# A cross-attention round on one core: both halves of the scores in one run, the exponentials ahead of the output's copy, Wo's product one round later

## What is computed

```python
x = x + cross_attention(ctx, layernorm(x), mask, ...)   # 8 heads of 64; queries from x, keys and values from x and ctx
x = x + int8_linear(layernorm(x))                       # rows quantised to 8 bits, times weight_q
x = x + attention(layernorm(x) @ We, ctx) @ W2.T        # softmax over tokens
x = x + routed_ffn(layernorm(x))                        # argmax of 8 experts, 128 -> 512 -> 128
```

```python
q, k, v = x_hat @ Wq, [x_hat, ctx_hat] @ Wk, [x_hat, ctx_hat] @ Wv
q, k = l2norm(q) * q_scale, l2norm(k) * k_scale      # per head
attn = softmax(where(mask, 8 * q @ k.T, -max))       # 128 queries, 128 + 77 keys, 8 heads
out = layer_norm((attn @ v) @ Wo)
```

## Time and profile before

| | |
|---|---|
| median of three runs | 973.37 us |
| span of the profiled execution | 950.6 us |
| median less the span: what lies around it | 22.8 us |
| TensorE busy, matmuls / weight loads | 96% / 84% |
| VectorE, ScalarE, POOL busy | 78%, 73%, 48% |
| TensorE's granted clock | full in nearly all slices |
| DMA | 31.44 MB, mean 33 GB/s |

### The profile page before, as it was taken

How to read it: one execution, slowest core, us unless ns; L and a number is a source line. 1 busy time by engine, 2 the same in 40 slices (tenths; PEclk the granted TensorE clock), 3 DMA queues, 4 the chain that set the end, 5 groups by cost and what they waited for, 6 DMA issues and landing times.

```text
span 950.6 us, 30821 instructions
## 1 busy us (share of the span) xinstructions
PE 912.8 (96%) x11286; PEld 794.5 (84%) x11286; DVE 744.9 (78%) x2526; ACT 693.5 (73%) x1671; POOL 458.1 (48%) x1094
## 2 busy tenths in 40 slices
PE   7999999999999999999999999999999999899997
PEld 6788888788878887888788878888888878898997
DVE  5566787888888888888888888888888978877553
ACT  4877777677778787778777777777778766676664
POOL 5422433354535453545354444444454545777554
PEclk9999999999999999999999999999999999999999
DMA  7743000000000000000000000000000022245310
GB/s 196 200 124 57 2 2 2 2 13 2 14 2 14 2 14 2 13 3 10 5 10 5 8 8 8 7 8 7 8 8 8 7 47 71 61 97 106 95 55 20
DMA packets 45193, 31.44 MB, mean 33 GB/s; under 512 B 11555, under 2 KB 40166, under 8 KB 45046
## 3 DMA queue, kind: packets, MB, share of 16 engines
q1 hardware_dynamic: 39398, 19.93, 9.2%
q0 software_dynamic: 4320, 8.50, 2.8%
q10 hardware_dynamic: 1328, 1.06, 0.4%
HBM read 17.75 MB, written 12.17 MB: 31 GB/s over the span
## 4 chain that ended last, share of the span: by engine, by line
PE 69%; DVE 14%; ACT 8%; issue 3%; POOL 3%; DMA 1%; SPq 1%; DVEq 0%; POOLq 0%; ACTq 0%
PE ps L1670 9%; PE ps L1717 9%; PE ps L1643 7%; PE ps L1765 6%; PE ps L1450 5%; PE ps L1622 5%; PE ps L1630 5%; PE ps L1452 5%; PE ps L1451 5%; DVE sumsq L1267 4%; PE ps L1722 3%; ACT probs L604 2%; PE ps L1749 2%; ACT qk_hat L617 2%; PE ps L1496 1%
## 5 line engine op out<-in xcount | busy, mean ns | idle before, releaser
L1374 DVE TENSOR_TENSOR qk_hat<-ps,rstd 128x512 f32<-128x512 f32 x168 | 106.3, 684 | 49.2 <-POOL rstd L870 49.1
L1267 DVE TENSOR_REDUCE sumsq<-qk_hat 128x8 f32<-128x512 f32 x168 | 107.8, 677 | 35.9 <-ACT qk_hat L617 34.7
L863 POOL TENSOR_TENSOR rs_t<-rs_y 128x32 f32<-128x32 f32 x73 | 17.9, 245 | 235.2 <-ACT rs_y L658 235.2
L1670 PE MATMUL ps<-v_x,prob 128*64 128x65 f32 x2048 | 127.9, 225 | 2.1 <-ACT w_all L568 0.4
L1670 PE MATMUL ps<-v_c,prob 128*64 128x65 f32 x2048 | 124.2, 222 | 0.0
L677 ACT ACTIVATE prob<-ps,neg_shift 128x512 f32<-128x512 f32 x128 | 88.4, 690 | 48.6 <-PE ps L1717 48.6
L1670 PEld LDWEIGHTS ps<-v_x,prob 128*64 128x64 f32 x2048 | 105.0, 137 | 20.9 <-issue 19.2
L617 ACT ACTIVATE qk_hat<-ps 128x512 f32<-128x512 f32 x168 | 98.5, 599 | 31.7 <-PE ps L1452 25.8
L1450 PE MATMUL ps<-w_hi,xc_hi 128*128 128x512 f32 x272 | 120.8, 444 | 0.8 <-POOL xc_lo L835 0.8
L1717 PE MATMUL ps<-qT_all,kT_all 64*128 64x128 f32 x1536 | 111.6, 285 | 2.3 <-ACT prob L677 1.1
L1452 PE MATMUL ps<-w_hi,xc_lo 128*128 128x512 f32 x272 | 107.3, 395 | 0.0
(11 more groups left out here) (245 smaller groups left out, 2257.2 us busy)
## 6 DMA issues: line engine op xcount, KB each, us to landing
x_res<-sorted_rows SPq DMA_DIRECT2D x71, 65.5 KB, 1.9
w_all<-in_L_ffn_W_dram SPq DMA_DIRECT2D x16, 256.0 KB, 5.3
sorted_rows<-fill SPq DMA_DIRECT2D x8, 327.5 KB
out_dram<-prob,x_res POOLq DMA_INDIRECT x71
sorted_rows<-stage,idx POOLq DMA_INDIRECT x64, 2.4
ctx_res<-in_ctx_dram SPq DMA_DIRECT2D x8, 115.5 KB
x_res<-in_x_dram SPq DMA_DIRECT2D x1, 768.0 KB
sorted_rows<-fill SPq DMA_DIRECT2D x1, 524.0 KB, 5.0
```

The costliest lines, as they stand in the source:

```text
L1267: nc.vector.reduce_sum(sumsq[:, n * H:(n + 1) * H], sq[:, n * INNER:(n + 1) * INNER].rearrange("p (h d) -> p h d", d=DH), AX).then_inc(ss_ ...
L1374: nc.vector.tensor_tensor(qk_hat[:, n * INNER:(n + 1) * INNER].rearrange("p (h d) -> p h d", d=DH), ps_qk[:, n, :].rearrange("p (h d) -> p ...
L1670: last = nc.tensor.matmul(dst[half:half + DH, :], prob[:, kt, col + half:col + half + DH], v, start=kt == 0, stop=kt == 1)
```

## The change

- `scores(1)` now follows `scores(0)` at once. It waits for `on_done` (VectorE has read banks 3 and 4), and its two units go to banks 4 and 3 in place of 4 and 6, so that the four units of scores have four banks.
- Where the context half is made in quarters of the array, the x half is too: 32 matmuls in place of 16. The fence increment between the two forms is gone.
- The flips of `o_n` go to bank 6, behind both halves and behind the first exponential; the flips of `xc_hat` go behind them.
- ScalarE does all four exponentials (0, 1, 3, 2), then `outputs_copied`, then `scaled_tokens`.
- Wo's product of block j-2 is in round j, behind the flips of `qk_hat` and slot a, in place of block j-1's at the end of round j. It waits for `ot_done` and `xct_sb`.
- Slot a waits at its head for the third exponential of the round before (bank 3), or, from block 65 on, for the copy of the output.

```diff
-        ps_v, ps_ot = (ps[:, 6, :], ps[:, 5, :]), ps[:, 3, :]
-        ps_s = (ps[:, 6, :], ps[:, 5, :], ps[:, 4, :], ps[:, 6, :])
+        ps_v = (ps[:, 6, :], ps[:, 5, :])
+        ps_s = (ps[:, 6, :], ps[:, 5, :], ps[:, 4, :], ps[:, 3, :])
...
+        def ps_ot(j, inside):
+
+            return ps[:, 6 if has(j, inside) else 3, :]
...
-                    nc.scalar.activation(o_t[:, :], ps_ot, ACT.Copy).then_inc(ot_done, 1)
+                    nc.scalar.activation(o_t[:, :], ps_ot(j, inside), ACT.Copy).then_inc(ot_done, 1)
...
+                if has(j, inside):
+                    exps((1, 3, 2))
+                if has(j - 1, inside) and not tail(j, inside):
+                    outputs_copied()
                 if inside or j != -2:
                     scaled_tokens()
-                if has(j - 1, inside) and not tail(j, inside):
-                    outputs_copied()
-                if has(j, inside):
-                    exps((1, 3, 2))
...
             def slot_a(j, rho, g, inside):
 
+                if has(j - 1, inside):
+                    pe.wait_ge(exp_done, 4 * j - 1)
+                elif has(j - 2, inside):
+                    pe.wait_ge(ot_done, j - 1)
...
                 slot_a(j, rho, g, inside)
+                if has(j - 2, inside):
+
+                    pe.wait_ge(ot_done, j - 1)
+                    if not has(j + 1, inside) and has(j - 3, inside):
+                        pe.wait_ge(o_cent, j - 2)
+                    if has(j + 1, inside):
+                        pe.wait_ge(xct_sb, j + 2)
+                    for t in range(PAIRS):
+                        last = nc.tensor.matmul(ps_o, o_t[:, t * P:(t + 1) * P], wo_sb[:, t, :],
+                                                start=t == 0, stop=t == PAIRS - 1)
+                    last.then_inc(wo_done, 1)
...
+                    same = halves(pos)[0] == halves(pos)[1]
...
-                            if kt == 0 or halves(pos)[0] == halves(pos)[1]:
+                            if same:
...
-                                    keys = k_t[rows, kept(n), t * P + key:t * P + key + DH]
+                                    keys = k_t[rows, 0 if kt == 0 else kept(n), t * P + key:t * P + key + DH]
...
                     scores(0)
+                if has(j - 1, inside):
+                    pe.wait_ge(on_done, j)
+                elif has(j, inside):
+                    pe.wait_ge(s["w_copied"], 6)
+                if has(j, inside):
+                    scores(1)
+                if has(j - 1, inside):
+
+                    if has(j, inside):
+                        pe.wait_ge(exp_done, 4 * j + 1)
+                    for t in range(PAIRS):
+                        last = nc.tensor.transpose(ps_ot(j, inside)[:, t * P:(t + 1) * P], o_n[:, t * P:(t + 1) * P], ident[:, :])
+                    last.then_inc(onT_done, 1)
                 seven_emptied(j, rho, g, inside)
...
-                if has(j - 1, inside):
-
-                    pe.wait_ge(on_done, j)
-                    for t in range(PAIRS):
-                        last = nc.tensor.transpose(ps_ot[:, t * P:(t + 1) * P], o_n[:, t * P:(t + 1) * P], ident[:, :])
-                    last.then_inc(onT_done, 1)
-                if has(j, inside):
-
-                    pe.wait_ge(exp_done, 4 * j + 1)
-                    if halves(pos)[0] != halves(pos)[1]:
-                        pe.sem_inc(s["fence_t"], 1)
-                    scores(1)
-                if has(j - 1, inside):
-
-                    pe.wait_ge(ot_done, j)
-                    if not has(j + 2, inside) and has(j - 2, inside):
-                        pe.wait_ge(o_cent, j - 1)
-                    if has(j + 2, inside):
-                        pe.wait_ge(xct_sb, j + 3)
-                    for t in range(PAIRS):
-                        last = nc.tensor.matmul(ps_o, o_t[:, t * P:(t + 1) * P], wo_sb[:, t, :],
-                                                start=t == 0, stop=t == PAIRS - 1)
-                    last.then_inc(wo_done, 1)
```

More of the change, by code:

```diff
@@ L1637, in run, with flipped @@
             def run(j, par, rho, g, inside, pos, turn):
-                if has(j, inside):
-                    for n in range(3) if fresh(pos) else range(2):
-                        pe.wait_ge(scaled, 3 * j + 1 + n)
-                        for t in range(PAIRS):
-                            last = nc.tensor.transpose(ps_qk[:, n, t * P:(t + 1) * P],
-                                                       qk_hat[:, n * INNER + t * P:n * INNER + (t + 1) * P], ident[:, :])
-                        last.then_inc(qkT_done, 1 if n == 0 or fresh(pos) else 2)
-                slot_a(j, rho, g, inside)
+                def flipped(n):
+                    pe.wait_ge(scaled, 3 * j + 1 + n)
+                    for t in range(PAIRS):
+                        last = nc.tensor.transpose(ps_qk[:, n, t * P:(t + 1) * P],
+                                                   qk_hat[:, n * INNER + t * P:n * INNER + (t + 1) * P], ident[:, :])
+                    last.then_inc(qkT_done, 1 if n == 0 or fresh(pos) else 2)
+                if has(j, inside):
+                    flipped(0)
+                    flipped(1)
+                if has(j, inside) and fresh(pos):
+                    flipped(2)
+                slot_a(j, rho, g, inside)
+                if has(j - 2, inside):
[8 more added lines that the diff above has]
+                    last.then_inc(wo_done, 1)
                 if tail(j, inside):
```

## The result

The changed kernel took 1025.26 us, the median of four runs (1022.74 to 1026.37), beside 972.62 for the kernel before (970.62 to 974.88): a ratio of 1.0525, with a 95% interval of 1.0497 to 1.0553. That is slower by 52.6 us; 37 had been forecast, and the range reached to 1027.

The account below looks back on a forecast made before the run. TensorE, busy 96% of the span, was taken to set the pace. 13 groups of four rounds at 2.58 us (33.5) plus 3.5 for earlier rounds gave +37 us, 1010 us; range 977 to 1027.

Parts of the forecast that it names:

- VectorE behind Wo: VectorE's round opens on Wo's product, so a later Wo delays everything queued there; 0.85 us later in round A.
- VectorE starts L1289 at S+5.97: Round A: VectorE's first statistics of Wo's product start 5.97 us after the round's first scores, in place of S+5.12.
- A, B, C and D: Four neighbouring profiled rounds, each starting at its first scores, time S; forecast +0.84, 0, +0.93, +0.81 us, sum 2.58.
- The eleven rounds before: I take half.: Rounds ahead of the 13 repeating groups, with less second-stage work: half the loss, 11 x 0.32 = 3.5 us.
- ScalarE's copies: `o_t` and `xc_t` come after four exponentials, so `xc_t` ends at S+4.86 and Wo waits 0.60 us in round A.
- Wo out of the latency of `qk_hat` in C: Round C: Wo's 0.99 us, formerly done during the wait for `qk_hat`, now follows it; v starts 0.78 us later.
- The quartered scores and the fence: 32 score matmuls for 16 in half the rounds cost 0 (bound 0.1 us a round); dropping the fence increment gives 0.
- Only Wo's own waits: Rival: only TensorE's waits at Wo count, 1.45 x 13, about +19 us; 978 to 990 us, chance 0.12.
- Faster, the copies land in time: Rival: `o_t` and `xc_t` end under flips and slot a, winning 9 to 15 us; 961 us, chance 0.12.
- No change: Rival: new waits of a quarter of the forecast size balance the gains; 973 us, chance 0.05.
- the quartered scores by their count: Rival: 16 more matmuls in each of 32 rounds at 34 ns add 17 us; 1027 us, chance 0.01.
- 950.6 us and 22.8 us lie around it: Profiled span of the kernel before, and the rest up to its median 973.4, left as they are.

Follow-up runs that it names:

- e4: The changed kernel with VectorE's token statistics and aggregates ahead of its wait for Wo; 998.83 us, ratio 1.0254 to the kernel before.
- e6: e1 with VectorE's token statistics and aggregates ahead of its wait for Wo, as in e4; 989.85 us, ratio 1.0149 to the kernel before.
- e5: e4 with ScalarE's order exponentials 0, 1, 3, the copies, then exponential 2; 989.58 us, ratio 1.0137 to the kernel before.
- e9: e6 with Wo put back ahead of the flips in the one round of four with rho 2; 982.35 us, ratio 1.0054 to the kernel before.
- e1: The kernel before with only Wo's product moved behind the next round's flips and slot a; 1016.94 us, ratio 1.0459.
- e7: e1 with Wo put back ahead of the flips in the one round of four with rho 2; 1001.58 us, ratio 1.0245 to the kernel before.
- e3: The kernel before with both halves of the scores quartered where the context half was, and no fence increment; 972.50 us, ratio 1.0004.

## Why the prediction was right in direction and too small in size

**VectorE behind Wo** was named as the main path, and it is: e4 and e6 take 26 and 30 us of the loss away by changing nothing but VectorE's order. The waits come at the places named: `xc_t` ahead of Wo in A and D, `o_c` at slot b, the one-hot, `o_n` ahead of C's second scores.

**The step that was mis-sized: "VectorE starts L1289 at S+5.97".** It took Wo's end as the distance from its start to the next product's (0.99), with 0.07 us to hand over, 1.06 in all. But VectorE began 1.23, 1.16, 1.16 and 1.24 us after Wo's start in A, B, C and D, 0.35 us after the *next* product's start each time. Wo itself came as forecast in A and D (S+4.90, forecast 4.91) and a little late in B (S+5.27 for 5.09) and C (S+6.28 for 6.18). The product behind it still came at S+6.08 in B (6.08) and S+7.09 in C (7.17), since Wo took 0.81 us up to its successor and not 0.99. So VectorE was at S+6.13, S+6.43, S+7.44 and S+6.14 where 5.97, 6.15, 7.24 and 5.97 stood; and what hangs on it followed:

| | forecast | measured |
|---|---|---|
| A, one-hot product | S+9.32 | S+9.49 |
| B, slot b (6.08 + 0.07 + 1.48) | S+7.63 | S+7.96 |
| C, `q_bf` done | S+9.77 | S+9.99 |
| D, slot b | S+7.50 | S+7.68 |
| rounds A, B, C, D | +0.84, 0, +0.93, +0.81 | +1.02, +0.34, +1.13, +0.96 |
| four rounds | +2.58 | +3.45 |

VectorE's later starts, 0.16, 0.28, 0.20 and 0.17, sum to 0.81, beside the 0.87 us by which the four rounds exceed the forecast. Of these 0.55 are the time from Wo's start to VectorE's, and the rest is mainly Wo's own later start in B and C. The row of Wo in the earlier trace rows had the first part: it gives 1.16 us as the duration, and the text had taken the distance to the next start. With 1.16 in place of 0.99 the forecast for A would have been S+6.14. For TensorE's own pace the distance is right; for who reads the product the row's end came far nearer.

**"The eleven rounds before: I take half."** There are twelve beside the 13 groups. 3.5 us were forecast and 7.65 measured, 0.64 a round where the later ones lose 0.82. That half was a guess, with no row under it. VectorE's wait for Wo and Wo's for `xc_t` are there from the first rounds on (19.0 and 4.5 us up to 165 us); the one-hot's isn't yet. The 51 later rounds gave +42.0 in place of 33.5. Sum: 42.0 + 7.65 + 1.2 = 50.8 against 37; the other 1.8 us aren't placed.

**The range reached the result by luck.** Its upper end of 1027 is called the sum with the bounds added. But 1010.4 + 3.2 (0.1 us in 32 rounds) + 3.9 (0.3 us in 13 groups) + 3.5 (full loss in the first rounds) is 1021. The last 6 us have no term, and the measured 1025.26 lies in them. What was really missing, VectorE's later start, is in none of the bounds.

**ScalarE's copies.** That `xc_t` ends at S+4.86 was right to 0.1 us (S+4.75 and S+4.76 in A and D; Wo, which waits for it, starts at S+4.90). Its price with VectorE's order mended, e4 to e5, is 11 us.

**Wo out of the latency of `qk_hat` in C** was right in kind; e6 to e9 price it at 9 us, e1 to e7 at 21 with VectorE's share in it. These prices don't add up: e1 alone has 44 of the 52.6 us, since one late Wo delays several things of which the last one counts.

**The quartered scores and the fence** at nothing: right, by e3. The rule of the Trainium skill (TensorE: Matmul & The Clock Gate, Wait — 56ns, not 53.3ns?) of about 62 ns per matmul does not bind here: round A of the changed kernel has 64 of them in 2.20 us, 34 ns each. The page gives that figure only for decoding in microcode, and no run shows how this chip decodes; so the rows set the price aside, and the prediction goes too far where it says that they contradict it.

**The rivals.** *Only Wo's own waits* (978 to 990 us) falls: e1 has no wait for `xc_t` and is 44 us slower. *Faster, the copies land in time* falls for the same reason, not only because they were 0.66 and 0.75 us late: in e1 they are in time, and VectorE still waits 73.6 us for Wo. *No change* and *the quartered scores by their count* fall with the result and with e3. The Trainium skill (Perfetto Trace Analysis, Identifying the Most-Contended Engine) judges TensorE's headroom by the weight loads' busy share, and by the matmul work done over the peak. The busy share fell from 84% to 77% here while the kernel got slower; it tells how much idle time there is, and not what it takes to win it. The other measure was not taken here.

**"950.6 us and 22.8 us lie around it"** was a wrong reading, though it cost the forecast nothing. The stretch from the last round's first flips to the end was not the usual one in that execution. Of the kernel before and of e3, whose code is the same there (windows; columns: busy time of each engine with its instructions, granted clock, DMA share, GB/s):

```profile
772.00:832.00 60.00, 53.80 (x569) 49.04 (x567) 49.70 (x190) 39.47 (x139) 38.71 (x63) 1.00 0.28 69
832.00:892.00 60.00, 58.21 (x522) 56.64 (x522) 43.26 (x175) 40.94 (x157) 41.93 (x49) 1.00 0.49 101
892.00:950.60 58.60, 51.82 (x465) 51.63 (x463) 27.81 (x102) 35.00 (x133) 29.30 (x30) 0.98 0.17 48
```

```profile
770.00:830.00 60.00, 51.27 (x521) 47.57 (x520) 42.90 (x168) 36.08 (x127) 33.11 (x57) 0.94 0.27 65
830.00:890.00 60.00, 47.67 (x403) 44.22 (x401) 35.79 (x153) 29.89 (x114) 36.57 (x45) 0.97 0.39 78
890.00:971.30 81.30, 72.05 (x627) 71.67 (x627) 39.82 (x145) 49.49 (x188) 39.22 (x41) 0.96 0.20 54
```

From the first flips of round 63 (770.32, 768.06 and 821.11) to the end it took 180.3 us in the kernel before, 203.2 in e3 and 203.2 in the changed kernel. In nearly every later run the time was 1.7 to 1.9 us more than the span (972.99 for 971.3 in e3), so the profiled execution of before lasted some 952 us, less than any timed one. The two spans, 73.7 us apart, overstate the loss; the marks up to round 63 don't. One difference shows in the traces: waits that the profile puts down to no engine of this core, such as

```profile
845.00 0.60 ACT L668 ACTIVATE tb_t<-ps 128x512 f32<-128x512 f32 x1 [4.76 <-remote]
```

in e3, where ScalarE waits 4.76 us for a releaser that is only called remote, and TensorE then 2.98 us for ScalarE. Such waits come to 24 to 32 us over all engines in each of the eleven later traces, and there are none in that of the kernel before. The granted clock was also fuller there. What they waited for is left open.

## What to carry to other kernels

Before a product is moved, ask who opens its round with a wait for it. Here everything in VectorE's queue moved along, though that engine is busy only 78% of the time, and putting independent work ahead of the wait won back 26 us, as much as the whole reorder was to bring. Look also for a product that fills another's latency: Wo cost nothing extra in the C rounds where it stood, and 9 us over the kernel, some 0.6 us a C round, once it was moved. And in a sum, use the distance between starts for the pace of TensorE, and the end of the row plus 0.1 us for the moment at which another engine begins to read the product.

## What was not expected of the hardware

- VectorE's first instruction on Wo's product started 0.10 to 0.11 us after the end of Wo's row (552.36 + 1.13 to 553.59; 564.94 + 1.06 to 566.10; 579.04 + 1.06 to 580.20; 590.80 + 1.13 to 592.04), though TensorE had begun its next product 0.24 to 0.25 us before that end. The ends of matmul rows are modelled by the profile, so this is a distance within it; the 1.16 to 1.24 us from start to start is what was recorded.
- Two executions of the same last stage differed by 23 us (180.3 and 203.2), at granted clocks of 0.98 to 1.00 and of 0.94 to 0.97; the first has no wait for a remote releaser, the second (e3) 32.4 us of them over all engines.
